# Attention with the next block's k (and first q) products in the tail of the current block, and a second layer whose run 1 multiplies the skip input before its norm

## The chip, the core and the metric

The kernel runs on one core of one Trainium2 chip. The metric is the device time of one execution in microseconds (us). TensorE is PE here (its weight loads are PEld), VectorE is DVE, ScalarE is ACT, GpSimd is POOL, and SyncE (SP) issues the DMAs.

## What is computed

Four conditioned layers follow each other on x of 32 sequences x 64 tokens x 256 channels, all in f32. Layers 0 and 2 are attention and MLP, layers 1 and 3 are selective state-space layers (32 and 64 states) run forward and backward. Of layer 0:

```python
normed = _adaln(x, cond, w_adaln1, b_adaln1)
q = (normed @ wq.T + bq).reshape(B, L, NH, HD)      # 16 heads of 16
k = (normed @ wk.T + bk).reshape(B, L, NH, HD)
v = (normed @ wv.T + bv).reshape(B, L, NH, HD)
attn = softmax(einsum('blhd,bmhd->bhlm', q, k) / scale)
x = x + einsum('bhlm,bmhd->blhd', attn, v).reshape(B, L, D) @ wo.T + bo
x = x + gelu(_adaln(x, cond, w_adaln2, b_adaln2) @ w1.T + b1) @ w2.T + b2
```

Layer 2 has a causal mask and gates on both additions, and its q, k and v have no bias. In layer 1 the part that matters here is `y = scan(...) + Dp * x`, where x is the convolved input; `Dp * x` is the skip input.

## The kernel before, in words

Channels lie on the partitions (256 channels are two chunks of 128), tokens along the free dimension. The 2048 tokens are four blocks of 512, and a block has four pairs of sequences. `attention(l)` is written once for each engine (PE, ACT, DVE, POOL) as a loop over blocks i. Each iteration interleaves three jobs: the attention of block i (`now`), the MLP of block i-1 (`mlp`), and the norm that makes the attention input H of block i+1 (`nxt`). Each engine executes its list strictly in the order written; `attention_steps` lists the same order, so that a name such as `k0@2` stands for a semaphore count. `made(engine, name)` waits for such a count, and `claim(bank, reader)` makes a product wait until the last reader of its PSUM bank is done.

On PE an iteration i of 1 to 3 is: `k0 k1` (L1250, through L1243), `ln2_mean`, `next_mean`, `q0 q1`, `ln2_var`, `v0` (L1262), `score0` (L1278), `v1`, `next_var`, `score1`, `up0` to `up3`, `score2`, `tr0` (a transpose, L1289), `up4`, `av0` (L1304), `up5` to `up7`, `score3`, `tr1`, first half of `down0` (L1326), `av1`, `tr2`, second half of `down0`, `av2`, `tr3`, first half of `down1`, `av3`, second half of `down1`, and `proj0 proj1` (L1243). I call the part up to `up0` the head of the block and the part from `tr1` on its tail. Block 0 has no MLP beside it, so its tail is `tr1 av1 tr2 av2 tr3 av3 proj0 proj1`.

DVE adds `proj` to the residual (L2345 or L2353), makes `ln2_added`, centres, normalises (`ln2_normed` L2366, `ln2_h` L2443) and works on the scores: `seen{p}` (L2379) adds the mask to `score{p}`, then come row maximum, subtraction, and after ACT's exponential the sum and its reciprocal (L2394). POOL expands the keys with the head mask (`kbd{p}`, four instructions, L2713) and multiplies by the reciprocal (`norm{p}`, L2721), for which `tr{p}` waits. ACT evicts k and q (L1828) and v (L1844), squares (L1833), computes the exponentials (L1863), evicts `tr{p}` as `pt{p}` (L1867) for `av{p}` and `av{p}` as `o{p}` (L1873). H is written by DVE's `next_h` (L2482), which waits for `v1` since v is the last reader of the old H. In block 0 of the first layer ACT also copies modulation sums (`site_copied`, L1857).

`pipeline(l)` is layer 1 or 3: eight runs (four blocks, forward and backward), each of 32 or 64 states in four steps. Each step is one DVE scan (L2255); POOL multiplies each finished state (L2678), and PE adds the products up. Work beside the scans (norm, convolution, next inputs) is placed at step numbers by `Plan`. On POOL, `skip` (L2546) makes the skip input in two halves, and `norm` makes `scaled` (L2563) and `h` (L2571). In the odd runs the convolution (L2059) overwrites its input and waits for `skip1`; DVE's `normed` (L2028) waits for `scaled`.

## Time and profile before

| | us |
|---|---|
| median of 3 runs (lowest, highest) | 4480.66 (4478.26, 4488.74) |
| the profiled execution, its own time | 4482.45 |
| its span in the trace | 4480.6 |
| PE busy | 4244.2 (95%) |
| DVE busy | 4059.0 (91%) |
| ACT busy | 3941.2 (88%) |
| POOL busy | 3821.8 (85%) |

The span is what lies between the first and the last recorded instruction; 1.85 us lie around it. The first layer's attention takes about the first 290 us, the second layer's scans run from 290 to 1629 us, the third layer's attention from about 1640 to 1950 us, and the fourth layer to the end. A timeline row has the start, the time of the group and, in brackets, how long the engine had been idle and what released it. TensorE has two clock levels, 2.4 GHz and 1.2 GHz; the column PEclk gives the granted share (1.00 or 0.50 of full speed).

### The profile page before, as it was taken

Reading aid. Unit: us, or ns where it says so; the run is one execution under the profiler, and the core shown is the slowest. Engines: PE = TensorE matmul, PEld = TensorE weight load, DVE = VectorE, ACT = ScalarE, POOL = GpSimd, SP = SyncE. Lnnn points to the kernel's source line nnn. Section 1 sums busy time; section 2 is a strip of 40 time slices with the busy share of each in tenths; the row PEclk is TensorE's granted clock in tenths of the full one; section 3 lists DMA queues with packets and bytes.
Section 4 is the critical chain, followed back from the end, with each engine's and each line's share of the span. In section 5 each row is a group of like instructions: output and inputs, shape, how many; then the busy total and the mean of one; then the engine's idle time right before and its main releaser. Section 6 shows DMA issues by size and latency. Waiting matters only on the chain.

```text
span 4480.6 us, 80902 instructions
## 1 busy us (share of the span) xinstructions
PE 4244.2 (95%) x31358; PEld 3461.6 (77%) x31358; DVE 4059.0 (91%) x3943; ACT 3941.2 (88%) x6176; POOL 3821.8 (85%) x1533
## 2 busy tenths in 40 slices
PE   9999899899899999999999999999999999999998
PEld 5458788788788864468888888888888888888887
DVE  6669999999999977669999999999999999999996
ACT  4569999999999964479989999999999999999995
POOL 3349999899899973259999999999999999999996
PEclk9999999999999999999999999999999999999999
DMA  4012122121121211032232422422422423323221
GB/s 166 1 30 65 61 66 65 53 64 64 53 64 66 64 65 41 1 60 69 94 69 80 82 67 78 82 70 81 87 70 74 79 78 93 65 75 69 72 82 40
DMA packets 241389, 303.33 MB, mean 68 GB/s; under 512 B 116448, under 2 KB 175712, under 8 KB 241008
## 3 DMA queue, kind: packets, MB, share of 16 engines
q1 hardware_dynamic: 241008, 298.15, 23.9%
q8 instruction: 251, 4.11, 0.4%
q14 instruction: 130, 1.06, 0.1%
HBM read 289.84 MB, written 8.26 MB: 67 GB/s over the span
## 4 chain that ended last, share of the span: by engine, by line
PE 41%; ACT 38%; DVE 13%; issue 5%; POOL 3%; DMA 0%; DVEq 0%; SPq 0%; POOLq 0%; ACTq 0%
PE psum L1137 11%; PE psum L1121 10%; ACT weights_c L1744 10%; PE psum L850 8%; ACT work L1765 7%; ACT work L1744 6%; DVE work L2255 6%; ACT weights_c L1765 6%; PE psum L1243 5%; DVE weights_c L2255 3%; PE psum L1118 2%; ACT L1461 2%; ACT modulation L1744 2%; POOL work L2678 1%; PE psum L1326 1%
## 5 line engine op out<-in xcount | busy, mean ns | idle before, releaser
L2678 POOL TENSOR_TENSOR work<-work,weights_a 128x2048 f32<-128x2048 f32 x512 | 1980.7, 3881 | 36.7 <-DVE work L2255 34.2
L2255 DVE TENSOR_TENSOR_SCAN work<-weights_c,psum 128x512 f32<-128x512 f32 x1316 | 1507.2, 1202 | 55.9 <-PE psum L1121 39.1
L1137 PE MATMUL psum<-ident,work 128*128 128x128 f32 x8192 | 1232.7, 274 | 13.1 <-POOL work L2678 12.6
L2678 POOL TENSOR_TENSOR weights_c<-weights_c,weights_a 128x2048 f32<-128x2048 f32 x256 | 990.7, 3879 | 13.8 <-DVE weights_c L2255 12.4
L1121 PE MATMUL psum<-ident,work 128*128 128x128 f32 x5464 | 952.4, 277 | 44.8 <-DVE weights_c L2255 13.3
L1137 PEld LDWEIGHTS psum<-ident,work 128*128 128x128 f32 x8192 | 963.8, 142 | 19.6 <-POOL work L2678 19.1
L1744 ACT ACTIVATE work<-work,decay 128x504 f32<-128x504 f32 x1172 | 819.0, 709 | 46.8 <-DVE weights_c L2255 25.6
L1121 PEld LDWEIGHTS psum<-ident,work 128*128 128x128 f32 x5464 | 659.6, 142 | 237.2 <-issue 130.6
L1121 PE MATMUL psum<-ident,weights_c 128*128 128x128 f32 x4432 | 782.6, 278 | 47.8 <-DVE work L2255 28.0
L2255 DVE TENSOR_TENSOR_SCAN weights_c<-work,psum 128x512 f32<-128x512 f32 x586 | 677.5, 1202 | 23.5 <-PE psum L1121 21.4
L2255 DVE TENSOR_TENSOR_SCAN work<-work,psum 128x512 f32<-128x512 f32 x586 | 675.9, 1201 | 25.2 <-PE psum L1121 16.9
L1121 PEld LDWEIGHTS psum<-ident,weights_c 128*128 128x128 f32 x4432 | 535.5, 142 | 173.0 <-issue 81.1
L1137 PE MATMUL psum<-ident,weights_c 128*128 128x128 f32 x4096 | 619.3, 274 | 9.4 <-POOL weights_c L2678 9.2
L1765 ACT ACTIVATE work<-work 128x512 f32<-128x512 f32 x683 | 486.0, 712 | 13.5 <-PE psum L1326 13.5
L1137 PEld LDWEIGHTS psum<-ident,weights_c 128*128 128x128 f32 x4096 | 483.5, 142 | 13.3 <-POOL weights_c L2678 13.1
L1765 ACT ACTIVATE work<-weights_a,work 128x512 f32<-128x512 f32 x683 | 486.1, 712 | 0.0
L1744 ACT ACTIVATE weights_c<-work,decay 128x504 f32<-128x504 f32 x584 | 409.2, 708 | 21.1 <-DVE work L2255 11.3
L1744 ACT ACTIVATE weights_c<-weights_a,weights_c 128x504 f32<-128x504 f32 x512 | 354.3, 707 | 35.4 <-DVE work L2255 34.3
L1744 ACT ACTIVATE weights_c<-work,weights_c 128x504 f32<-128x504 f32 x512 | 355.3, 708 | 23.9 <-DVE work L2255 23.4
L2255 DVE TENSOR_TENSOR_SCAN weights_c<-weights_c,psum 128x512 f32<-128x512 f32 x292 | 342.1, 1202 | 7.4 <-PE psum L1121 6.0
L1765 ACT ACTIVATE weights_c<-work,weights_c 128x512 f32<-128x512 f32 x384 | 273.1, 712 | 2.4 <-PE psum L1209 2.4
L1765 ACT ACTIVATE weights_c<-weights_a,weights_c 128x512 f32<-128x512 f32 x384 | 272.8, 710 | 0.0
(230 smaller groups left out, 6198.3 us busy)
## 6 DMA issues: line engine op xcount, KB each, us to landing
weights_a<-c_rows SPq DMA_DIRECT2D x384, 512.0 KB, 3.7
work<-b_diagonals SPq DMA_DIRECT2D x240, 128.0 KB, 2.4
weights_c<-b_diagonals SPq DMA_DIRECT2D x112, 128.0 KB, 2.5
b_diagonals<-weights_c SPq DMA_DIRECT2D x1, 4096.0 KB, 18.2
weights_c<-in_L_cond_fwd_in_w SPq DMA_DIRECT2D x8, 512.0 KB, 5.4
weights_c<-in_L_cond_fwd_xproj_w SPq DMA_DIRECT2D x4, 1024.0 KB, 7.0
weights_c<-in_L_cond_bwd_in_w SPq DMA_DIRECT2D x8, 512.0 KB, 5.3
weights_c<-in_L_cond_bwd_xproj_w SPq DMA_DIRECT2D x4, 1024.0 KB, 7.1
```

The lines of the kernel that those rows point to most:

```text
L850: last = nc.tensor.matmul(PS[0:rows, bank, :], weights[k], moving[k], start=(k == 0), stop=(k == len(moving) - 1))
L1118: nc.tensor.matmul(PS[:, bank, SCALED * P:T], buf["dtx"][r % 2][:, SCALED, j * P:(j + 1) * P], buf["diagonal"][:, s // 2 % 2, s % 2, :], s ...
L1121: last = nc.tensor.transpose(PS[:, bank, t * P:(t + 1) * P], buf["scaled"][s % INPUTS][t][:, j * P:(j + 1) * P], IDENT[:, :])
L1137: last = nc.tensor.matmul(PS[:, i, k * P:(k + 1) * P], flat[:, at:at + P], IDENT[:, :], start=begins and k == 0, stop=ends and k == DC - 1 ...
L1243: last = nc.tensor.matmul(PS[:, bank, :], weights[k], moving[k], start=(k == 0), stop=(k == len(moving) - 1))
L1326: last = nc.tensor.matmul(PS[:, 5 + c, :], W2A[:, k, c * P:(c + 1) * P], G[l][:, k, :], start=(k == 0), stop=(k == MLP // P - 1))
L1461: act.add_instruction(mybir.InstLoadActFuncSet(name=nc.get_next_instruction_name(), engine=act.engine, act_func_set_id=which, ins=[], outs ...
L1744: f(seqs[:, :, lo:lo + SEQ - 1], dts[:, :, lo:lo + SEQ - 1], ACT.Exp, scale=rate).then_inc(ss["decay_ready"], 1)
L1765: last = f(buf["scaled"][s % INPUTS][t], buf["dtx"][r % 2][:, t, :], ACT.Copy, scale=weight)
L2255: v.tensor_tensor_scan(buf["ring"][s % RING][:, along, j], buf["decay"][q % DECAYS[l]][:, along], PS[:, 4 + q % LOOKAHEAD, along], 0.0, AL ...
L2678: g.tensor_tensor(state, state, row.unsqueeze(2).broadcast_to([P, T, DC]), ALU.mult).then_inc(ss["prod_ready"], 1)
```

## The change

In both attention layers, for i of 0 to 2, the next block's k products are moved from the head of iteration i+1 into the tail of iteration i: for i of 1 and 2, `k0@i+1` stands between `av1` and `tr2` and `k1@i+1` between `av2` and `tr3`; for i = 0 both stand between `av2` and `tr3`, followed by `q0@1` after `tr3` and `q1@1` after `av3`. These products use PSUM banks 0 and 1. ACT's evictions move with them. The heads are reordered: block 1 has `v0` (bank 6), the two means, `v1` (bank 2), `score0`, `ln2_var`; blocks 2 and 3 have `q0 q1`, the two means, `v0` (bank 6), `score0`, `ln2_var`, `v1`. ACT's square of the next input no longer stands behind the evictions of q. `site_copied(4)` moves on ACT from before `pt2` to behind `o2`. In the second layer's run 1, POOL makes `skip0` and `skip1` after its first and second state, ahead of `scaled`, instead of between `scaled`, `h` and the convolution. No product is added or removed. The lists in `attention_steps` change in the same way and are left out below.

```diff
--- before.py
+++ after.py
@@ -229,7 +229,7 @@
         if norms:
             a += ["square"] if not (first and gated) else []
             v += ["mean", "normed"]
-            g += ["scaled", "skip0", "h", "skip1"] if r % 2 else ["scaled", "h"]
+            g += ["skip0", "skip1", "scaled", "h"] if r == 1 else ["scaled", "skip0", "h", "skip1"] if r % 2 else ["scaled", "h"]
         if head and r % 2 == 0:
             a += ["bc"]
         if r == RUNS:
...
@@ -1247,10 +1283,20 @@
                     def average(name, bank, reads, added):
                         product(name, bank, reads, [MEAN[:, :]], [added[:, 0, :]])
 
-                    def project(name, c, at, bank):
+                    opens, second, more = now and i == 0, i == 1, now and i + 1 < NBLK
+
+                    def project(name, c, at, bank, block=i):
                         o = at * D + c * P
-                        product(f"{name}{c}", bank, by("act", f"{name}{c}"),
-                                [WQKVO[:, k, o:o + P] for k in range(KC)], [H[:, k, :] for k in range(KC)])
+                        claim(bank, (st["act"].semaphore, st["act"].lead(f"{name}{c}@{block}")))
+                        for k in range(KC):
+                            last = nc.tensor.matmul(PS[:, bank, :], WQKVO[:, k, o:o + P], H[:, k, :],
+                                                    start=(k == 0), stop=(k == KC - 1))
+                        last.then_inc(mine.sem(f"{name}{c}@{block}"), 1)
+
+                    def upcoming(name, c, at):
+                        if more:
+                            made("dve", f"next_h@{i}")
+                            project(name, c, at, c, i + 1)
 
                     def values(half, bank):
                         wv = WQKVO[:, :, 2 * D:3 * D].rearrange("p k (h r d) -> p k h r d", r=2, d=HD)
@@ -1332,21 +1378,23 @@
                         if l == 0 and i == 0:
                             site_sums(s, (7, 6, 5)[s % 3])
 
-                    if now:
+                    if opens:
                         behind("out1")
-                        if l == 2 and i == 0:
+                        if l == 2:
                             pe.wait_ge(pipe[1]["pool"].semaphore, pipe[1]["pool"].lead(f"h@{RUNS - 1}"))
+                            pe.wait_ge(dma_w[2], 16 * NW[2])
                         else:
                             made("dve", f"next_h@{i - 1}")
-                        if i == 0:
-                            if l == 0:
-                                pe.wait_ge(dma_qkv, 16 * 4)
-                                pe.wait_ge(dma_small, 16 * 2)
-                            else:
-                                pe.wait_ge(dma_w[2], 16 * NW[2])
+                            pe.wait_ge(dma_qkv, 16 * 4)
+                            pe.wait_ge(dma_small, 16 * 2)
                         for c in range(KC):
                             project("k", c, 1, c)
                         behind("mean")
+                    if now and i > 1:
+                        for c in range(KC):
+                            project("q", c, 0, 2 + c)
+                    if second:
+                        values(0, 6)
                     ahead("in1", "in1")
                     if mlp:
                         if l == 0 and i == 1:
@@ -1358,9 +1406,16 @@
                     if nxt:
                         made("dve", f"next_added@{i}")
                         average("next_mean", 4, by("dve", "next_centred"), NEXT_A[1])
-                    if now:
+                    if opens:
                         for c in range(KC):
                             project("q", c, 0, 2 + c)
+                    if now and i > 1:
+                        values(0, 6)
+                    if second:
+                        values(1, 2)
+                    if now and i > 0:
+                        made("act", f"q1@{i}")
+                        score(0)
                     if l == 0 and i < 0:
                         pe.wait_ge(dma_cond, 16 * 2)
                         site_sums(0, 0)
@@ -1372,10 +1427,11 @@
                     if l == 0 and i == NBLK:
                         site_sums(6, 4)
                     behind("var")
-                    if now:
+                    if opens:
                         values(0, 4)
                         made("act", f"q1@{i}")
                         score(0)
+                    if now and not second:
                         values(1, 2)
                     behind("gate2")
                     if nxt:
@@ -1423,16 +1479,25 @@
                         down(0, 0)
                     if now:
                         attend(1)
+                        if i > 0:
+                            upcoming("k", 0, 1)
                         turn(2)
                     if mlp:
                         down(0, 1)
                     if now:
                         attend(2)
+                        if i == 0:
+                            upcoming("k", 0, 1)
+                        upcoming("k", 1, 1)
                         turn(3)
+                        if i == 0:
+                            upcoming("q", 0, 0)
                     if mlp:
                         down(1, 0)
                     if now:
                         attend(3)
+                        if i == 0:
+                            upcoming("q", 1, 0)
                     if mlp:
                         down(1, 1)
                     if now:
@@ -1822,11 +1887,17 @@
 
                     second_lead = l == 0 and i == NBLK
 
-                    def project(name, dst, bank):
-                        for c in range(KC):
-                            made("pe", f"{name}{c}")
+                    opens, second, more = now and i == 0, i == 1, now and i + 1 < NBLK
+
+                    def project(name, dst, bank, chunks=range(KC), block=i):
+                        for c in chunks:
+                            act.wait_ge(st["pe"].semaphore, st["pe"].lead(f"{name}{c}@{block}"))
                             f(dst[:, c, :], PS[:, bank + c, :], ACT.Identity,
-                              bias=vec(cfg["b" + name], c)).then_inc(done(f"{name}{c}"), 1)
+                              bias=vec(cfg["b" + name], c)).then_inc(mine.sem(f"{name}{c}@{block}"), 1)
+
+                    def upcoming(name, dst, *chunks):
+                        if more:
+                            project(name, dst, 0, chunks, i + 1)
 
                     def square(name, centred, to):
                         made("dve", f"{name}_centred")
@@ -1885,24 +1956,32 @@
                             tables(EXP_LN)
 
                     behind("yt")
-                    if now:
+                    if opens:
                         project("k", KF, 0)
+                    if now and i > 1:
+                        project("q", Q, 2)
+                    if second:
+                        values(0, 6)
                     behind("square")
                     ahead("mirror1", None)
                     if mlp:
                         square("ln2", LN_A[0], LN_A[1])
                     ahead("mirror3", "silu_x")
-                    if now:
+                    if opens:
                         project("q", Q, 2)
+                    if second:
+                        values(1, 2)
                     if nxt:
                         square("next", NEXT_A[0], NEXT_A[1])
+                    if now and i > 1:
+                        values(0, 6)
                     behind("rstd")
                     if mlp:
                         rsqrt("ln2", 7, LN_A[2])
-                    if now:
-                        if i == 0:
-                            act.wait_ge(vbd_zeroed, 1 + l // 2)
+                    if opens:
+                        act.wait_ge(vbd_zeroed, 1 + l // 2)
                         values(0, 4)
+                    if now and not second:
                         values(1, 2)
                     if nxt:
                         rsqrt("next", 4, NEXT_A[2])
@@ -1930,12 +2009,21 @@
                         turned(1)
                         exps(3)
                         outputs(1)
-                        site_copied(4, 6)
+                        if i > 0:
+                            upcoming("k", KF, 0)
                         turned(2)
                         outputs(2)
+                        site_copied(4, 6)
+                        if i == 0:
+                            upcoming("k", KF, 0)
+                        upcoming("k", KF, 1)
+                        turned(3)
+                        if i == 0:
+                            upcoming("q", Q, 0)
+                        outputs(3)
+                        if i == 0:
+                            upcoming("q", Q, 1)
                         site_copied(5, 5)
-                        turned(3)
-                        outputs(3)
                     if i == 1:
                         rates = A1 if l == 0 else A3
                         act.wait_ge(dma_rates, 16 if l == 0 else 16 * 3)
@@ -2588,9 +2676,12 @@
                     if 0 <= r < RUNS and r % 2 == 0:
                         yield from skip(r, done)
                     if norm1:
+                        if r == 1:
+                            yield from skip(r, done)
                         yield from norm(r, plan, done, 2 if head else 4, H, nb, f"z3@{r - 1}" if r > 0 else None,
-                                        between=skip(r, done, (0,), 13))
-                        yield from skip(r, done, (1,), 17)
+                                        between=skip(r, done, (0,), 13) if r > 1 else ())
+                        if r > 1:
+                            yield from skip(r, done, (1,), 17)
                     if ends:
                         yield from norm(r, plan, done, 3, H1B, nb, f"up2@{r - 1}" if r >= 4 else None)
                     if r % 2 and head and r >= 0:
```

## Rows read from the trace of the kernel before

**Rows 1.** The page, section 4: shares of the chain that ended last, by engine.
```profile
PE 41%; ACT 38%; DVE 13%; issue 5%; POOL 3%; DMA 0%; DVEq 0%; SPq 0%; POOLq 0%; ACTq 0%
```
**Rows 2.** Waits of PE, 122 to 181 us: who was waited for, total us, times, longest.
```profile
PE psum L1289 <- POOL work L2721: 1.8, 2, 1.1
PE psum L1304 <- ACT work L1867: 0.4, 1, 0.4
```
**Rows 3.** Timeline of PE, block 2: start us, us, what, count, [idle before, releaser].
```profile
121.90 3.60 PE L1243 MATMUL psum<-work,weights_a 128*128 128x512 f32 x8
125.33 3.60 PE L1243 MATMUL psum<-normed,weights_a 128*128 128x512 f32 x8
...
134.87 2.02 PE L1262 MATMUL psum<-weights_a,normed 128*64 128x128 f32 x32
136.81 1.09 PE L1278 MATMUL psum<-work 64*64 64x256 f32 x16
137.84 2.02 PE L1262 MATMUL psum<-weights_a,normed 128*64 128x128 f32 x32
...
165.95 1.07 PE L1289 MATMUL psum<-ident,work 128*128 128x128 f32 x8 [0.66 <-POOL work L2721]
...
172.17 1.06 PE L1289 MATMUL psum<-ident,work 128*128 128x128 f32 x8 [1.10 <-POOL work L2721]
```
**Rows 4.** Timeline of ACT, block 2: the square of the next block's centred input.
```profile
134.70 1.05 ACT L1833 ACTIVATE work<-work 128x1024 f32<-128x1024 f32 x1
```
**Rows 5.** Timeline of DVE, block 2: `ln2_normed`, `ln2_h`, `next_normed`.
```profile
137.02 1.23 DVE L2366 TENSOR_TENSOR work<-work 128x1024 f32<-128x1024 f32 x1 [0.55 <-ACT work L1839]
...
139.42 1.52 DVE L2443 TENSOR_TENSOR work<-work,modulation 128x1024 f32<-128x1024 f32 x1
...
149.52 1.63 DVE L2366 TENSOR_TENSOR work<-work 128x1024 f32<-128x1024 f32 x1
```
**Rows 6.** Timeline of PE, first layer, tail of block 0, `proj`, `k` of block 1.
```profile
54.52 1.11 PE L1304 MATMUL psum<-work 128*32 128x64 f32 x32 [2.87 <-ACT work L1867]
...
61.57 5.07 PE L1243 MATMUL psum<-work,weights_a 128*128 128x512 f32 x8 [0.84 <-ACT work L1873]
66.47 3.60 PE L1243 MATMUL psum<-normed,weights_a 128*128 128x512 f32 x8
```
**Rows 7.** Timeline of ACT, the same stretch: the six evictions of `site_copied(4)`.
```profile
52.29 1.17 ACT L1857 ACTIVATE modulation<-psum,vectors 128x32 f32<-128x32 f32 x6
```
**Rows 8.** Timeline of DVE, the same stretch: `next_h` of block 0.
```profile
53.41 1.16 DVE L2482 TENSOR_TENSOR normed<-work,modulation 128x1024 f32<-128x1024 f32 x1
```
**Rows 9.** Two windows: busy time (instructions) of each engine, PEclk, DMA share, GB/s.
```profile
54.20:64.30 10.10, 6.89 (x76) 4.57 (x77) 0.37 (x1) 3.52 (x12) 2.58 (x2) 0.50 0.67 206
1696.00:1709.60 13.60, 7.67 (x76) 4.87 (x77) 5.94 (x5) 2.81 (x6) 2.75 (x1) 0.50 0.89 304
```
**Rows 10.** Timeline of PE, third layer, tail of block 0, and `k` of block 1.
```profile
1696.69 1.10 PE L1304 MATMUL psum<-work 128*32 128x64 f32 x32 [2.53 <-ACT work L1867]
1701.08 1.94 PE L1289 MATMUL psum<-ident,work 128*128 128x128 f32 x8 [3.29 <-POOL work L2721]
...
1711.36 3.60 PE L1243 MATMUL psum<-normed,weights_a 128*128 128x512 f32 x8
```
**Rows 11.** Timeline of DVE, the same stretch: `next_h` of block 0.
```profile
1699.21 2.80 DVE L2482 TENSOR_TENSOR normed<-work,modulation 128x1024 f32<-128x1024 f32 x1
```
**Rows 12.** Timeline of POOL, second layer, run 1: `scaled`, then `skip1`.
```profile
468.66 1.91 POOL L2563 TENSOR_TENSOR scratch<-scratch,modulation 128x1024 f32<-128x1024 f32 x1
...
486.87 2.11 POOL L2546 TENSOR_TENSOR work<-work,vectors 128x1024 f32<-128x1024 f32 x1
```
**Rows 13.** Timeline of DVE, the same run: `normed`, then the first convolution instruction.
```profile
471.63 1.22 DVE L2028 TENSOR_TENSOR scratch<-scratch,psum 128x1024 f32<-128x1024 f32 x1 [0.27 <-ACT psum L1500]
...
489.09 0.81 DVE L2059 TENSOR_SCALAR work<-psum,vectors 128x512 f32<-128x512 f32 x1 [2.88 <-POOL work L2546]
```
**Rows 14.** Timeline of POOL, block 2: the four instructions of `kbd2`.
```profile
138.02 3.39 POOL L2713 TENSOR_TENSOR work<-work,head_mask 128x256 f32<-128x256 f32 x4 [4.37 <-PE psum L1278]
```

More of the change, by code:

```diff
@@ L397, in attention_steps @@
         add(act, mlp, *(f"gelu{j}" for j in range(4, 8)))
-        add(act, now, "exp2", "o0", "pt1", "exp3", "o1", "pt2", "o2", "pt3", "o3")
+        add(act, now, "exp2", "o0", "pt1", "exp3", "o1")
+        if i > 0:
+            upcoming(act, "k0")
+        add(act, now, "pt2", "o2")
+        upcoming(act, *(("k0", "k1") if i == 0 else ("k1",)))
+        add(act, now, "pt3")
+        if i == 0:
+            upcoming(act, "q0")
+        add(act, now, "o3")
+        if i == 0:
+            upcoming(act, "q1")
         add(dve, mlp, *sums("x"), "ln2_added")
```

43 lines of the change are left out of this document (35 added, 8 removed).

## The prediction

> **What bounds the kernel now.** I read the chain of work that ended last first: PE and ACT share it, DVE has a third of either [rows 1]. So no engine is the bound alone, and each stage needs its own reading. The change touches two stages (attention in layers 0 and 2) and one run of layer 1's scans; the scan stages otherwise keep every instruction.
>
> In attention, blocks 1 to 3 repeat one pattern. The waits of PE over block 2 show it almost full: 2.2 us in 59, two in the tail before `tr2` (0.66) and `tr3` (1.10), where PE waits for POOL's `norm`, and 0.4 before `av0` [rows 2, 3]. The reader is to see that the tail, which is to take 3.43 us more of PE work per block, has 1.76 us of room. The head has none: `proj` starts at 121.90 and nothing idles up to `up0`. The tail of block 0, without MLP, has more room (a gap of 2.87 us in layer 0, of 3.29 in layer 2), but there PE runs at the lower of its two clocks [rows 6, 9, 10].
>
> **The ledger.** The change removes and adds no product, so PE's work is the same in sum. What it moves, it takes from one place of PE's queue and puts into another. The end of a layer's attention moves by the change of PE's idle time, plus what the clock costs. k is four 512-column products in two chunks, 125.33 - 121.90 = 3.43 us for a set of this size, 1.71 a chunk [rows 3]; q is the same.
>
> **Head of blocks 2 and 3.** From the start of `proj`: `proj` to 3.43, `q` to 6.86, the two means to 8.58 (each half of a chunk, 0.86), `v0` 1.94 (134.87 to 136.81 [rows 3]), `score0` 1.03 (136.81 to 137.84), so `ln2_var` ends at 12.4 instead of at 134.87 - 121.90 = 12.97. It is hardly earlier, because q only takes k's place as cover for DVE's residual. After it come Ln and Exp on ACT. Before, they also stood 0.75 us behind the square (134.70 to 135.75, the variance ready at 134.87 plus a hand-over of 0.2 [rows 4]), and `ln2_normed` began at 137.02, 2.15 after the variance; now about 1.5 after it, at 13.96. From `ln2_normed` to the end of `ln2_h` DVE takes 139.42 + 1.45 - 137.02 = 3.85 us, `seen0` between them [rows 5], so `ln2_h` is made at 17.8 and `up0` can start at 17.9. PE on its side is through `v1`, `next_var` and `score1` at 12.4 + 1.94 + 0.86 + 1.1 = 16.4. So a new wait of 1.5 us stands ahead of `score1` and `up0`: DVE's chain is late next. Behind it 0.2 more goes at `up3` (behind the first gelu) and 0.4 at `tr1`, since `norm1` follows DVE, which gained less than PE. With the 0.4 at `av0`, which stays, that is 2.5 us.
>
> Block 2 fills both tail gaps (1.76): 2.5 against 2.14 (0.38 + 0.66 + 1.10), so it is **0.4 us longer**. Block 3 gives k away and takes none, so it keeps the 1.10 gap and, as `tr1` is late, 0.24 of the 0.66: -3.43 + (2.5 + 1.34 - 2.14) = **-1.7 us**.
>
> **Head of block 1.** k and q are both gone, and DVE's residual is covered by `v0` only: `ln2_mean` at 5.4, `ln2_var` from 10.07 to 10.97. ACT's queue is now `v0`, square, `v1`, square: Ln waits for the second square until 11.35 and `ln2_normed` begins at 12.7, `ln2_h` ends at 16.5. PE is ready at 12.95: a wait of 3.7 us, plus 0.2 and 0.4 as above. The block is -6.86 + 3.43 + (3.67 + 0.2 + 0.38 + 0.39 - 2.14) = **-0.9 us**. Layer 2 does each residual in two DVE instructions, one more of 0.7 us per chunk: 0.4 us of further wait in block 1 and 0.1 in 2 and 3. Sum of the three blocks: **-2.2 us in layer 0, -1.6 in layer 2**.
>
> **Tail of block 0, layer 0.** `site_copied(4)` no longer stands ahead of `pt2`: 1.0 us [rows 7], so `av2` starts at 53.5. But `k0@1` reads H, and `next_h` ends at 53.41 + 1.16 = 54.57 [rows 8]: PE waits until 54.7, and `tr3` is queued behind k. PE's clock is low from 54.2 to 64.3 [rows 9]; it came back 2.8 us after dense products had begun at 61.57 [rows 6]. With the dense k starting at 54.7 I let it come back 2.9 us later, at 57.6: 1.43 us of work are done by then, the other 2.0 end at 59.57. Then `tr3` 0.9 (the work at full clock behind the rows of 172.17), `q0` 1.71, which hides `pt3` on ACT (an instruction of the 1.05 us class [rows 4]), `av3` 0.6 (1.11 at the low clock [rows 6]), `q1` 1.71, which hides `o3`: `proj` starts at 64.55 and ends at 67.98, against 66.47 [rows 6]: **+1.5 us**.
>
> **Tail of block 0, layer 2.** `next_h` runs from 1699.21 to 1702.01 [rows 11], while `tr3` started at 1701.08 [rows 10]. Put ahead of it, k waits for `next_h` until 1702.15 and delays `tr3`, `av3` and `proj` behind it. PE idles 4.4 us instead of 3.29 there. The clock is low from 1696 to 1709.6 [rows 9]; after dense work from 1702.15 I let it return at 1706.2, 4.05 us later (between the 2.8 us of layer 0 and the bound below). k ends at 1707.6, `tr3` 1708.5, `q0` 1710.2, `av3` 1710.9, `q1` and then `proj` from 1712.6 to 1716.0, against 1711.36 [rows 10]: **+4.65 us**.
>
> The two ends of the clock: if it stays low through all of k in both tails, k and q cost up to 1.7 us more in each layer (+3.4); if it does not fall at all, 1.4 less in layer 0 and 2.0 less in layer 2. The rows have it fall while PE idles ahead of `av2`, in work that the change leaves as it is, so I take the middle. The Trainium skill (TensorE: Matmul & The Clock Gate, "What's actually happening") says that the throttled state is the default and activity releases it; by that rule, too, only the idle stretch ahead of k decides, and this case's rows show the fall there. A denser tail would by the rule be the better end, 3.4 us less.
>
> **Run 1 of layer 1.** DVE's first convolution instruction waited 2.88 us for `skip1` [rows 13]; POOL had it behind `scaled` and `h`. With both skips of 2.0 us each ahead of `scaled`, that wait goes. But POOL was full there but for two gaps of 0.64 us ahead of its second and third state, so `scaled` ends 4.1 - 1.3 = 2.8 us later: 468.66 + 1.87 + 2.8 = 473.4 [rows 12]. DVE's `normed`, at 471.63 before, needs it and now starts at 473.45: a new wait of 1.8 us, with two scans that PE and ACT have ready queued behind it. Net 1.8 - 2.88 = **-1.1 us**. The ends: -2.9 if `scaled` is in time, +1.8 if the wait that is removed was only hiding another.
>
> No DMA is moved; SP's queue waits only for scan counts and is not passed.
>
> **Sum.** Layer 0: 1.5 - 2.2 = -0.7. Layer 2: 4.65 - 1.6 = +3.0. Run 1: -1.1. Together +1.2 us on a span of 4480.6, so 4481.8 in the trace and 4483.7 for an execution like the profiled one; that one was 1.8 above the median, so a median of **4481.9 us**. Everything else costs nothing: kbd0 and kbd1 of the next block move under `down1` and `proj`, where POOL was idle.
>
> **A rule against it.** DVE's next `normed` takes 1.63 us beside POOL's `kbd3`, and 1.23 where POOL is idle [rows 5]. `kbd2`, four instructions in 3.39 us [rows 14], started 1.0 us after `ln2_normed`; now `score0` comes earlier and `kbd2` covers `ln2_normed` (+0.4) while `ln2_h`, 1.45 beside POOL, gets free (-0.3). I take 0. The Trainium skill (SBUF — State Buffer, "SBUF: two separate sides") has these two engines share one port pair as an exclusive lock: a VectorE instruction with two SBUF inputs waits for the whole GpSimd instruction in flight. The 0.4 us agree with it; what it would cost at its worst is rival B.
>
> **Rivals.** (A) *The gain is real*: the new head waits do not come, because DVE gets through from `ln2_mean` to `ln2_h` as PE does. For it speaks that DVE idles several times in the head (0.55 before `ln2_normed` [rows 5]); against it, that this chain is of dependent steps, not of busy time. It takes away 6.7 us in layer 0 and 7.3 in layer 2 (3.7 and twice 1.5 each, plus the 0.6 of layer 2), and with `scaled` in time 1.8 more: 4481.9 - 15.8 = 4466.
>
> (B) *Slower by the lock of DVE and POOL*: in each of six heads `ln2_normed` comes while one of `kbd2`'s instructions is in flight and waits for its whole 3.39 / 4 = 0.85 us, on the path to `up0`: 5.1 us, and 4487. It decides if `score0` starts less than 3.4 us ahead of `ln2_normed`; I have them 3.4 apart in block 2 (10.5 and 13.96) and 3.6 in block 1, on the edge. If in run 1 the removed wait also hid another (+2.9), 4490.
>
> (C) *The change does less than it says*: k in the tail is held by its bank (`seen3` must have read banks 0 and 1) or by `next_h`, and PE just idles at another place. In blocks 1 and 2 `seen3` ends within 0.3 us of `av1`, so at most 0.3 a block: 4482.5, not to be told from the forecast.
>
> **Chances.** Forecast with C 0.70, its own range 4477 to 4486; A or most of it 0.17; B or another loss of that size 0.13. The range of 4466 to 4490 reaches to both. A measurement of this kernel can tell about 0.3% (13.4 us) from no change: below 4467.2 is A at its full size, 0.10; above 4494.1 needs more than B, 0.05; within 0.85.
>
> **What would show it.** In PE's timeline: k between `av1` and `tr2` with no gap ahead of `tr2` and `tr3`; new waits of PE for DVE ahead of `score1` (L1278) and `up0`, 1.5 us in blocks 2 and 3 and 3.7 in block 1; `proj` of block 1's head ending 1.5 and 4.65 us later; blocks of 58.0, 59.3 and 57.2 us (58.9 before, at the full clock). In run 1, `skip1` ahead of `scaled`, DVE waiting some 2 us before L2028 and not at L2059. Wrong it would be if PE's head waits are under 0.5 us, if the clock does not fall in the tails, or if the fourth layer, whose instructions are the same, changes its length by more than a few us.

## The result, and the profile after

| | before | after |
|---|---|---|
| median of 8 runs each, in turn on one chip (us) | 4485.01 (4478.26 to 4489.28) | 4492.51 (4485.54 to 4499.36) |
| the profiled execution, its own time | 4482.45 | 4492.14 |
| its span in the trace | 4480.6 | 4490.3 |

The ratio is 1.0019, with an interval of 1.0011 to 1.0028: the change costs 7.5 us, where 1.2 were forecast. The kernel before also came out 4.3 us above the median of its first three runs, so part of the distance to the predicted 4481.9 is the start from which it was counted; 6.3 us are the step's own. The range ended at 4490.0. Counted by the ratio from the first median, the time would be 4489.2; as measured it lies 2.5 us above the range.

The page of the kernel after: its span, the busy times, and section 4, which answers [rows 1].

```profile
span 4490.3 us, 80913 instructions
PE 4250.9 (95%) x31358; PEld 3463.1 (77%) x31358; DVE 4058.2 (90%) x3943; ACT 3942.1 (88%) x6176; POOL 3815.2 (85%) x1533
PE 41%; ACT 38%; DVE 12%; issue 5%; POOL 3%; DMA 0%; DVEq 0%; SPq 0%; POOLq 0%; ACTq 0%
```

The page hardly changes. PE's busy time grows by 6.7 us with the same number of instructions, and no other engine's grows by more than 1 us. That is the first hint: the products did not become more, some of them became slower.

I cut both traces at the starts of DVE's scans, which no step of the change moves. The stages of the two spans, in us:

| stage | before | after | difference |
|---|---|---|---|
| start to the first scan of layer 1 | 289.8 | 291.2 | +1.4 |
| layer 1, run 1 | 170.9 | 174.0 | +3.1 |
| layer 1, the other runs | 1168.8 | 1170.6 | +1.8 |
| last scan of layer 1 to first scan of layer 3 (layer 2) | 320.7 | 327.5 | +6.8 |
| layer 3's scans | 2479.2 | 2475.8 | -3.4 |

The last row needs care. Layer 3 has the same instructions in all kernels here, and their traces show lengths from 2474.6 to 2479.3, six of the thirteen near 2475.8 and four near 2479.2. Both of these occur with the old and with the new order in layer 2, so I don't take the row for an effect of the change. Of the +9.7 us in the spans, the reader should keep the +6.8 of layer 2 and the +3.1 of run 1.

Timeline of PE, after, third layer, from the tail of block 0 (answers [rows 10]) to the lead of layer 3:

```profile
1703.05 1.10 PE L1350 MATMUL psum<-work 128*32 128x64 f32 x32 [2.53 <-ACT work L1938]
1708.43 5.72 PE L1292 MATMUL psum<-normed,weights_a 128*128 128x512 f32 x8 [4.28 <-DVE normed L2570]
...
1719.11 3.60 PE L1279 MATMUL psum<-work,weights_a 128*128 128x512 f32 x8
...
1732.10 1.12 PE L1279 MATMUL psum<-work,mean_weights 128*128 128x512 f32 x2 [1.01 <-DVE work L2449]
1735.53 1.17 PE L1324 MATMUL psum<-work 64*64 64x256 f32 x16 [2.30 <-DVE work L2467]
1736.62 8.71 PE L1279 MATMUL psum<-work,weights_a 128*128 128x512 f32 x16
...
1908.65 1.12 PE L1279 MATMUL psum<-work,mean_weights 128*128 128x512 f32 x2 [1.39 <-DVE work L2449]
1910.09 19.10 PE L886 MATMUL psum<-work,weights_c 128*128 128x512 f32 x40 [0.31 <-ACT work L1742]
```

The same instructions of `up0` to `up3` and of layer 3's lead, before:

```profile
1727.89 7.13 PE L1243 MATMUL psum<-work,weights_a 128*128 128x512 f32 x16
1898.66 17.40 PE L850 MATMUL psum<-work,weights_c 128*128 128x512 f32 x40 [0.31 <-ACT work L1677]
```

Windows of after over three of these places (columns as in [rows 9]):

```profile
1704.00:1716.00 12.00, 7.72 (x26) 3.80 (x20) 4.31 (x4) 2.94 (x5) 4.98 (x5) 0.64 1.01 343
1735.00:1742.00 7.00, 6.47 (x25) 3.06 (x26) 6.93 (x8) 2.99 (x4) 0.35 (x1) 0.76 0.00 0
1908.00:1916.00 8.00, 7.04 (x12) 2.90 (x13) 4.69 (x5) 4.51 (x4) 0.00 (x0) 0.79 0.01 2
```

The first place is the forecast one: k waits 4.28 us for `next_h`. The second and third are not. Behind the new waits of block 1's head the granted clock is 0.76 in the mean of its window (a stretch at 1.2 GHz inside one at 2.4), and `up0` to `up3`, sixteen instructions in the trace, take 8.71 us. At 1910 the first products of layer 3, its lead (forty instructions), meet another low stretch (0.79) and take 19.10.

In the second layer's run 1, DVE's waits in the stretch 452 to 626 us (engine line waited for: us in total, times, longest):

```profile
DVE work L2343 <- PE psum L1157: 5.3, 8, 1.5
DVE scratch L2116 <- POOL scratch L2651: 2.0, 1, 2.0
```

The timeline of DVE there, `normed` and the first convolution instruction, which answer [rows 13]:

```profile
475.50 1.22 DVE L2116 TENSOR_TENSOR scratch<-scratch,psum 128x1024 f32<-128x1024 f32 x1 [1.96 <-POOL scratch L2651]
489.99 0.78 DVE L2147 TENSOR_SCALAR work<-psum,vectors 128x512 f32<-128x512 f32 x1
```

And that of POOL, `scaled`, which answers [rows 12]:

```profile
473.47 1.93 POOL L2651 TENSOR_TENSOR scratch<-scratch,modulation 128x1024 f32<-128x1024 f32 x1
```

`normed` waits 1.96 us for `scaled`, and the convolution no longer waits, both as forecast. But DVE's scans wait 5.3 us for PE in eight places; before it was 2.0 in three. The timeline of PE shows how: the same products at 512 and at 519 us.

```profile
512.40 0.85 PE L1157 MATMUL psum<-ident,weights_c 128*128 128x128 f32 x3
513.04 1.06 PE L1173 MATMUL psum<-ident,work 128*128 128x128 f32 x4
...
519.32 0.49 PE L1157 MATMUL psum<-ident,weights_c 128*128 128x128 f32 x3
519.65 0.60 PE L1173 MATMUL psum<-ident,work 128*128 128x128 f32 x4
```

PE's clock is low in three stretches of run 1 (497.4 to 500.8, 511.0 to 517.9, 528.1 to 531.5); before it was low in one, 491.1 to 497.9.

### The profile page after: what moved, and what is told of

It is laid out like the page before. It is cut to its first block, busy times and chain, and to the rows that moved or that the text cites. A ratio compares the mean times of both kernels' runs of the same rounds, so it can differ in the third digit from the quotient of the medians.

```text
span 4490.3 us, 80913 instructions
## 1 busy us (share of the span) xinstructions
PE 4250.9 (95%) x31358; PEld 3463.1 (77%) x31358; DVE 4058.2 (90%) x3943; ACT 3942.1 (88%) x6176; POOL 3815.2 (85%) x1533
## 4 chain that ended last, share of the span: by engine, by line
PE 41%; ACT 38%; DVE 12%; issue 5%; POOL 3%; DMA 0%; DVEq 0%; SPq 0%; POOLq 0%; ACTq 0%
PE psum L1173 11%; ACT weights_c L1809 10%; PE psum L1157 10%; PE psum L886 9%; ACT work L1830 7%; ACT work L1809 6%; ACT weights_c L1830 6%; DVE work L2343 5%; DVE weights_c L2343 3%; PE psum L1279 3%; PE psum L1154 3%; ACT L1526 2%; POOL work L2769 2%; PE psum L1372 2%; ACT modulation L1809 2%
## 5 line engine op out<-in xcount | busy, mean ns | idle before, releaser
L1173 PE MATMUL psum<-ident,weights_c 128*128 128x128 f32 x4096 | 618.6, 274 | 10.6 <-POOL weights_c L2769 10.3
```

What stands on the lines that cost most here:

```text
L1173: last = nc.tensor.matmul(PS[:, i, k * P:(k + 1) * P], flat[:, at:at + P], IDENT[:, :], start=begins and k == 0, stop=ends and k == DC - 1 ...
```

## The experiments

My theory after the result: *the waits are as forecast, and what they bring along is priced wrongly, namely TensorE's clock in the stretches behind them.* Rivals: the waits themselves add up to more than forecast; or the parts of the change disturb each other. All kernels but e7, e10 and e11 hold the same work as the two given ones; these three add products of no use, called fillers. The experiments share a table that chooses the order by layer, `MODE`, where "new" is the changed kernel's order and "old" the one before. A diff below shows only the line that tells a kernel from its neighbour; lists that change with it, such as POOL's, are left out. Each kernel's median is of 11 runs, and its ratio is taken against the kernel before, run beside it.

### One part at a time

e1 keeps the change of run 1 alone, both attentions have the old order:

```diff
-MODE = {0: 'new', 2: 'new'}
+MODE = {0: 'old', 2: 'old'}
```

e2 keeps both attentions and has the old order in run 1:

```diff
-g += ["skip0", "skip1", "scaled", "h"] if r == 1 else ["scaled", "skip0", "h", "skip1"] if r % 2 else ["scaled", "h"]
+g += ["scaled", "skip0", "h", "skip1"] if r % 2 else ["scaled", "h"]
```

e3 keeps layer 0's attention alone and e4 layer 2's alone, both with the old run 1:

```diff
-MODE = {0: 'new', 2: 'new'}
+MODE = {0: 'new', 2: 'old'}
```
```diff
-MODE = {0: 'new', 2: 'new'}
+MODE = {0: 'old', 2: 'new'}
```

> Only the order of the skip products in run 1 of layer 1 is changed; attention is that of the kernel before. Theory (the skip change is worth about 1 us, and what run 1 lost in the changed kernel's profile is TensorE at 1.2 GHz in that execution): DVE waits about 2 us for POOL's scaled at its normed and not at its first convolution, that convolution starts 0.5 to 1.5 us earlier after the start of run 1 than before (39.0 us), run 1 lasts 169 to 171 us unless the clock falls more often in it, and the whole is within 0.05% of the kernel before (-1 us). Rival (the skip order itself makes run 1 longer): run 1 lasts 174 us again as in the changed kernel, and the whole is 3 us slower.

> Both attention layers as in the changed kernel, run 1 of layer 1 in the old order. Theory (the loss is attention's): the whole is 6 to 9 us slower than before, run 1 lasts 171 us, layer 0 to its last proj is 0.4 us longer, layer 2 from the last scan of layer 1 to the first of layer 3 is 5 to 7 us longer (327 against 320.7). Rival (the skip change carries 3 us of the loss): 3 to 5 us slower than before.

> Only layer 0's attention is changed. Theory (layer 2 has the loss, since there next_h is late; layer 0 is even): within 0.05% of the kernel before, first scan at 290 to 291.5 us against 289.8. Rival (the head waits of blocks 1 to 3 make both layers alike slower): half the loss, 3 to 4 us slower, and the first scan at 293 us.

> Only layer 2's attention is changed. Theory: 5 to 7 us slower than before, all of it between the last scan of layer 1 and the first of layer 3, 4.9 us of it before the end of the first proj (k waits for next_h). Rival (both layers alike): 3 to 4 us slower.

| kernel | median us | ratio (interval) | run 1 | layer 2's stage |
|---|---|---|---|---|
| e1, run 1 alone | 4484.24 | 0.9997 (0.9989 to 1.0006) | 174.1 | 320.7 |
| e2, both attentions | 4491.02 | 1.0017 (1.0008 to 1.0025) | 170.9 | 327.5 |
| e3, layer 0's attention | 4483.79 | 0.9999 (0.9990 to 1.0007) | 170.9 | 320.8 |
| e4, layer 2's attention | 4491.15 | 1.0014 (1.0005 to 1.0023) | 171.2 | 327.5 |

The stages follow their part exactly: 327.5 wherever layer 2's attention is changed and 320.7 where it is not; 174.0 or 174.1 only where run 1 is. The parts don't disturb each other, and the loss that can be measured sits in layer 2. Layer 0's part changes nothing that can be measured, though in the traces of e2 and e3 layer 1 starts at 294.9 and 292.8 us and not by 291.5, as I had expected of e3; the section on layer 0 comes back to this. For run 1, e1's rival came true in the stage: it is 3.2 us longer there too, where I had expected 169 to 171 us. The whole of e1 is not slower all the same; a loss of 3 us is at the edge of what the ratio tells.

### Layer 2: who gets k early

In e5 block 0 keeps its own tail, and only from block 1 on does k move into the tail; block 1 then has the old head.

```diff
-MODE = {0: 'new', 2: 'new'}
+MODE = {0: 'old', 2: 'from1'}
```

> Only layer 2 is changed, and its block 0 takes nothing into its tail: block 1 has k and q in its head as before, blocks 1 and 2 give k away. Stage read: last scan of layer 1 to first scan of layer 3 (320.7 us before, 327.5 with all of layer 2 changed). Theory (block 0's tail, where k waits for next_h and runs at the low clock, and block 1's starved head are the loss): 321 to 323 us, and the whole 0 to 3 us slower than before. Rival (the reordered heads of blocks 2 and 3 lose it): 325 us or more.

The stage took 321.7 us, as expected, and the kernel 4486.19, a ratio of 1.0007 (0.9998 to 1.0016). So 5.7 of the 6.8 us go away when block 0 keeps its tail and block 1 its head; 1.7 of them are the low stretch in the lead of layer 3, which e5 does not have either. From one last `proj` of a block to the next, block 1 was 1.7 us longer than before (3.43 us of k into 1.76 us of room), block 2 was 0.7 longer and block 3 was 1.25 shorter: the steady part of the move brings 1.1 us of loss, not a gain.

e6 is e4 with k of block 1 behind `tr3` and q behind `av3`, so that `tr3` isn't queued behind the wait for `next_h`. The names stand for what follows `av2`, `tr3` and `av3`.

```diff
-FIRST = {2: (('k0', 'k1'), ('q0',), ('q1',))}
+FIRST = {2: ((), ('k0', 'k1'), ('q0', 'q1'))}
```

> Only layer 2 is changed; in block 0's tail k stands behind tr3 instead of ahead of it, and q behind av3. Theory (the moved products themselves fill PE at the low clock, whatever their order; the wait for next_h is only a little longer than the one for tr3 was): stage 326 to 327 us, 0.7 to 1 us less than 327.5. Rival (k, queued ahead of tr3 behind a late next_h, is the whole of the loss): 323 us.

PE, e6, the tail of block 0 and `score1` of block 1:

```profile
1703.61 1.94 PE L1354 MATMUL psum<-ident,work 128*128 128x128 f32 x8 [3.29 <-POOL work L2831]
1705.34 5.13 PE L1306 MATMUL psum<-normed,weights_a 128*128 128x512 f32 x8
...
1714.56 3.60 PE L1293 MATMUL psum<-work,weights_a 128*128 128x512 f32 x8
...
1730.97 1.09 PE L1343 MATMUL psum<-work 64*64 64x256 f32 x16 [2.30 <-DVE work L2489]
1732.06 8.83 PE L1293 MATMUL psum<-work,weights_a 128*128 128x512 f32 x16
```

The wait of k is gone and `tr3` waits its old 3.29 us, but `proj` starts only 0.7 us earlier than in the changed kernel (82.7 us behind the last scan, against 83.3). The 4.28 us wait was thus not the price of the tail: what k and q put ahead of `proj` is 6.9 us of work, and only the gaps of the old tail take some of it back. The stage took 325.2 us, 2.3 less than after (expected: 0.7 to 1 less); 1.7 of that is the low stretch in the lead of layer 3, which e6 doesn't have. The ratio is 1.0016 (1.0007 to 1.0025), not told apart from the changed kernel's.

### Layer 2: does the wait of the head cost the clock?

e7 is e4 with eight 128-column products ahead of `score1` in block 1, into a PSUM tile that nobody reads. They add 1.95 us of work of no use (sixteen instructions in the trace) into a wait of 2.30.

```diff
+                    if second or late:
+                        made("dve", f"ln2_squares@{i}")
+                        for _ in range(8 if second else 0):
+                            nc.tensor.matmul(PS[:, 5, 0:P], MEAN[:, :], MEAN[:, :], start=True, stop=True)
                     if now:
                         score(1)
```

> Only layer 2 is changed, and PE gets eight small products without a use (128 columns, MEAN by MEAN) ahead of score1 of block 1, where it waited 2.3 us for DVE. Theory (the starved head also lets the clock fall, and the four up products that follow pay 1.6 us for it): the clock stays at its upper level there, up0 to up3 take 7.1 instead of 8.7 us, and the stage is 1 to 1.8 us shorter than 327.5. Rival (the wait costs only itself): up0 to up3 as before, stage 327.5.

Timeline of PE, e7, the same place and the lead of layer 3:

```profile
1730.69 1.95 PE L1468 MATMUL psum<-mean_weights 128*128 128x128 f32 x16
1733.16 1.09 PE L1343 MATMUL psum<-work 64*64 64x256 f32 x16 [0.52 <-DVE work L2493]
1734.25 7.46 PE L1293 MATMUL psum<-work,weights_a 128*128 128x512 f32 x16
...
1906.75 17.41 PE L900 MATMUL psum<-work,weights_c 128*128 128x512 f32 x40 [0.31 <-ACT work L1764]
```

Windows of e7 over the two places (columns as in [rows 9]):

```profile
1732.00:1739.00 7.00, 6.48 (x33) 3.25 (x33) 6.93 (x7) 2.60 (x4) 0.00 (x0) 1.00 0.00 0
1905.00:1913.00 8.00, 7.38 (x17) 3.23 (x18) 4.51 (x5) 4.21 (x4) 0.00 (x0) 1.00 0.01 2
```

`score1` starts as late as ever, the clock stays at 1.00, and the ups take 7.46 us instead of 8.71 (I had expected 7.1). All four traces with this wait and no filler in layer 2 (after, e2, e4, e6) have the low stretch, and it starts 100.4 to 100.7 us behind the last scan of layer 1 in each. Up to the wait e7's clock ran as e6's did: in both the low stretch of the tail ended 76.5 us behind that scan. So the filler is what differs. Work without use made the stage shorter: 324.7 us against 327.5. Of the 2.8 us, 1.0 is block 1 (the ups gain 1.25, and 0.25 of it goes back into waits further on); 1.7 are the lead of layer 3, whose low stretch is absent as well. That second one is not a wait's doing: the 1.39 us wait in front of it stands in every kernel (1.38 in e7's). The low stretch is there in the traces of after, e2 and e4, which reach the lead 274.3 us behind the last scan of layer 1, and not in those of e5, e6 and e7, which reach it at 270.3, 273.8 and 273.2. I can say that it goes with where the stage's work falls in time, and not why. The ratio of e7 is 1.0004 (0.9995 to 1.0013), which overlaps that of e4, 1.0014 (1.0005 to 1.0023): the gain is seen in the stage, and the whole time doesn't settle it.

### Layer 0 with the same products

e10 is e3 with such products in all three heads; the diff is against e7's line.

```diff
-for _ in range(8 if second else 0):
+for _ in range(8 if second else 5):
```

> Layer 0's attention as in the changed kernel, with products without use (they write a PSUM tile that nobody reads) ahead of score1: 8 of them in block 1, 5 each in blocks 2 and 3; layer 2's attention and run 1 as in the kernel before. Theory (the wait of score1 lets TensorE's clock fall, and the ups pay): with TensorE at work during the 2.30 us wait the first ups of block 1 take about 7.1 us in place of the 8.9 of the changed kernel, and the last projection of layer 0 ends near 237.5 us (before 239.8, changed kernel 240.2). Rival (the low clock in block 1 has another cause): ups stay near 8.9 us and the last projection ends at 240 or later. The whole: between 0 and 3 us less than before.

Timeline of PE, e10, block 1, and below it the window of e10 over the tail and middle of block 0 (columns as in [rows 9]):

```profile
87.87 1.09 PE L1343 MATMUL psum<-work 64*64 64x256 f32 x16 [0.52 <-DVE work L2493]
88.95 7.46 PE L1293 MATMUL psum<-work,weights_a 128*128 128x512 f32 x16
```
```profile
37.50:61.40 23.90, 22.70 (x174) 19.27 (x173) 16.41 (x16) 8.48 (x21) 8.49 (x8) 0.50 0.37 141
```

The first half of the expectation held: the ups took 7.46 us instead of 8.93, and block 1 was 58.18 us long (71.94 to 130.12, from `proj` to `proj`), where the changed kernel had 60.2 and the forecast was 58.0. That the filler did it isn't shown here, since e2, with the same wait and no filler, has 7.46 and 58.18 as well. The second half failed: the last `proj` of layer 0 started at 247.0 us, not 237.5. The window says where it went: in block 0, whose instructions are those of e3 and of the changed kernel, the clock was low from 37.5 to 61.4 without a break. Traces taken apart in this way, in us:

| kernel | block 0: first `k` to end of `proj` | blocks 1 to 3: to last `proj` |
|---|---|---|
| layer 0 old: before | 49.72 | 173.15 |
| layer 0 old: e1 | 50.21 | 173.17 |
| layer 0 old: e4 | 50.08 | 173.15 |
| layer 0 old: e8 | 49.71 | 173.17 |
| layer 0 old: e9 | 50.43 | 173.15 |
| layer 0 old: e5, e6 and e7 | 54.97 | 173.17 |
| layer 0 new: after | 50.02 | 173.61 |
| layer 0 new: e3 | 51.34 | 172.57 |
| layer 0 new: e2 | 56.43 | 171.58 |
| layer 0 new, filler: e10 | 57.75 | 171.55 |
| layer 0 new, filler: e11 | 57.79 | 171.57 |

Block 0 has a short and a long form under either order. Blocks 1 to 3 are 1.6 us shorter than before with the clock up (e2, e10, e11), 0.6 shorter in e3 and 0.5 longer in after, where the clock fell behind `score1`. e2 also shows that the wait alone doesn't decide: it has no filler, and no low stretch there. What else decides is open.

### Run 1: how many skips ahead of `scaled`

e8 has both skips behind `scaled` and ahead of `h`; e9 has one ahead of `scaled` and one behind it. Attention is as before in both.

```diff
-["skip0", "skip1", "scaled", "h"]
+["scaled", "skip0", "skip1", "h"]
```
```diff
-["skip0", "skip1", "scaled", "h"]
+["skip0", "scaled", "skip1", "h"]
```

> Attention as in the kernel before; in run 1 of layer 1 POOL makes both skips right behind scaled and ahead of h. DVE's normed then has no wait for POOL, and the first convolution waits for h and its product, 0.8 us less than the 2.88 of before. Theory by waits alone: run 1 lasts 170.1 us (170.9 before, 174.0 in the changed order). Rival (the clock sets run 1's length: where the stall lies against the clock's falls decides): run 1 lasts 168 or 172 us or more, with one clock fall or three in it, whatever the waits say.

> The attention is that of the kernel before; in run 1 of the second layer one skip product stands ahead of scaled and one behind it (before: both behind it, after: both ahead of it). Theory (waits set run 1): scaled's product ends half as far back as in the changed kernel, so that normed on VectorE waits some 1 us less than the 1.96 us of the changed kernel, and the first convolution product on TensorE, which waited 2.88 us in the kernel before, waits some 0.9 us; run 1 takes 168.9 us, 2.0 less than the 170.9 before. Rival (the granted clock sets run 1): any product moved ahead shifts the stretches at low clock, as in the changed kernel with three falls, and run 1 takes 172 us or more although the wait is shorter. The whole: 2 us less than before, 0.04%, within what can be told, so the stage and its clock decide and not the ratio.

DVE's waits in run 1, for e8 and then for e9:

```profile
DVE work L2365 <- PE psum L1171: 3.7, 4, 1.7
DVE scratch L2138 <- ACT psum L1583: 0.3, 1, 0.3
```
```profile
DVE work L2365 <- PE psum L1171: 2.3, 4, 1.4
```

Timeline of DVE, e9, `normed`:

```profile
472.04 1.22 DVE L2138 TENSOR_TENSOR scratch<-scratch,psum 128x1024 f32<-128x1024 f32 x1 [0.25 <-ACT psum L1583]
```

The window from 484 to 530 us, for before, after and e9 in this order (columns as in [rows 9]):

```profile
484.00:530.00 46.00, 37.40 (x261) 31.74 (x260) 42.86 (x47) 37.74 (x61) 41.27 (x19) 0.93 0.17 58
```
```profile
484.00:530.00 46.00, 37.82 (x246) 32.68 (x244) 42.75 (x47) 36.00 (x58) 37.69 (x18) 0.87 0.17 55
```
```profile
484.00:530.00 46.00, 37.56 (x274) 31.09 (x275) 45.31 (x50) 39.98 (x65) 42.07 (x20) 1.00 0.18 58
```

Run 1 took 170.0 us in e8 (expected 170.1) and 168.5 in e9 (expected 168.9): neither `normed` nor the convolution waits for POOL in e9, and DVE is busy 45.31 of 46 us. The whole runs gave ratios of 1.0006 (0.9997 to 1.0014) and 1.0000 (0.9991 to 1.0009), so the 2.3 us are seen in the stage and not in the time. By its waits alone the changed order was worth 1.1 us, and its run 1 took 4.2 more than that, in the trace after and in e1's alike. The granted clock differs as well: 0.93 before, 0.87 in after and 1.00 in e9. That the clock is the whole cause is not shown: in e8 DVE's scans waited 3.7 us for PE in a run 1 without any low stretch. Why the clock fell three times in the changed order is open too. PE's idle spans in that stretch are much the same in after (the longest 1.51, 1.41, 1.32, 1.29 us) and in e9 (1.51, 1.44, 1.40, 1.32), and only the first has the falls. I tried no filler there, since a useless product would have needed a free PSUM bank between the scans.

### The gaining parts together

e11 is layer 0 of e10, layer 2 as before, and run 1 of e9.

> The parts that gained by the waits, put together: layer 0's attention as changed with the products without use ahead of score1, layer 2's attention as before, run 1 with one skip product ahead of scaled. Theory (parts add up): 2.3 us from layer 0 and 2.0 us from run 1, so 4 us below the kernel before, a ratio of 0.9991, and the last layer as before. Rival (an earlier start of layer 1 only shifts where the clock falls in the scans, which gives the gain back): ratio 1.0000 or above, with the first scan of layer 1 earlier but the stages behind it longer by as much.

DVE, e11, run 1:

```profile
532.63 2.33 DVE L2369 TENSOR_TENSOR_SCAN work<-weights_c,psum 128x512 f32<-128x512 f32 x2 [0.15 <-PE psum L1171]
535.47 1.22 DVE L2369 TENSOR_TENSOR_SCAN work<-weights_c,psum 128x512 f32<-128x512 f32 x1 [0.50 <-PE psum L1171]
```

4482.79 us, a ratio of 0.9999 (0.9990 to 1.0007), where 0.9991 was expected: no faster than before by any measurement made here. Its trace had the long block 0 and, in run 1, one low stretch (528.6 to 532.0) that e9's did not have, with DVE's waits above and 169.6 us instead of 168.5. So the gains of single stages are real in the traces and as large as the differences that the clock makes between traces. Nothing tried here beats the kernel before by an amount that can be measured.

## Why the prediction was wrong

The step that failed is the term for blocks 1 to 3 of layer 2: -1.6 us in the prediction, +1.9 measured. Of the 3.5 us between them, 2.7 are TensorE's clock, which fell in two places that the sum had at full clock. The other terms follow in the order of the sum.

**The ledger and the head.** Right in the main. The "new wait of 1.5 us" ahead of `score1` in blocks 2 and 3 was 1.40, released by DVE's `seen0`; in block 1, the wait of 3.7 was 1.01 ahead of `next_var` and 2.30 ahead of `score1`. Timeline of PE, after, block 2 (beside [rows 3]):

```profile
131.78 2.02 PE L1308 MATMUL psum<-weights_a,normed 128*64 128x128 f32 x32
133.73 1.09 PE L1324 MATMUL psum<-work 64*64 64x256 f32 x16
...
140.28 1.09 PE L1324 MATMUL psum<-work 64*64 64x256 f32 x16 [1.40 <-DVE work L2467]
```

Timeline of DVE, `ln2_normed` and `ln2_h` (beside [rows 5]):

```profile
137.30 1.62 DVE L2454 TENSOR_TENSOR work<-work 128x1024 f32<-128x1024 f32 x1 [1.07 <-ACT work L1910]
140.10 1.22 DVE L2531 TENSOR_TENSOR work<-work,modulation 128x1024 f32<-128x1024 f32 x1
```

`ln2_normed` starts 14.19 us behind `proj` (forecast 13.96), and from there to the end of `ln2_h` it is 4.02 us (forecast 3.85), so `up0` starts at 18.26 and not at 17.9. Blocks 2 and 3 of layer 0 took 59.4 and 57.5 us (59.3 and 57.2), and with the clock up blocks 1 to 3 were worth 1.6 us, against 2.2 forecast: each block was sized 0.2 us too short.

**Tail of block 0, layer 0.** The waits right, the clock wrong, and to the kernel's benefit. Timeline of PE, after (beside [rows 6]), then the window of the first row of [rows 9]:

```profile
54.22 3.70 PE L1292 MATMUL psum<-normed,weights_a 128*128 128x512 f32 x8 [0.48 <-DVE normed L2570]
...
62.89 3.60 PE L1279 MATMUL psum<-work,weights_a 128*128 128x512 f32 x8
```
```profile
54.20:64.30 10.10, 10.08 (x60) 5.12 (x61) 0.00 (x0) 6.19 (x18) 6.83 (x10) 1.00 0.72 226
```

The clock was 1.00 where it was 0.50 before, and the block was 0.3 us longer, not 1.5. But the other traces with this tail had 1.3, 1.5 and 2.8 us more than the old form of like length (51.34 against 50.08, 56.43 and 57.75 against 54.97), so that the forecast of 1.5 lies inside what they show, if traces of like length are the right pairs.

**Tail of block 0, layer 2.** Right: k waited 4.28 us (4.4), and `proj` ended 4.9 us later against the last scan (4.65). The sentence that k "delays `tr3`, `av3` and `proj` behind it" was right in fact and misleading as a reason: e6 took that delay away and got 0.7 us.

**Blocks 1 to 3 and the lead, layer 2.** This is the step that failed. Forecast -1.6; measured +0.8, +0.7, -1.3 and +1.7 in the lead, +1.9 in all. Of the 3.5 us between them, the low stretch behind `score1` is 1.0 (block 1 took 59.68 us in after and 58.67 in e7) and the one in the lead 1.7; the rest, some 0.8 us, is again 0.2 to 0.3 a block. The sentence that failed is "only the idle stretch ahead of k decides". I priced the clock only in the tails, where it was low before, and treated the new waits of the heads as their own length. A wait of 2.3 us cost 2.3 and then 1.25 in the work behind it, of which 1.0 stayed in the block. For the 1.7 in the lead the sum had no term, and what brings that low stretch stays open.

**Run 1.** The two waits were right (1.8 forecast, 1.96; the 2.88 gone). The net was -1.1 by them and +3.1 in the trace, with a lower clock, though here no run ties the clock to a wait or the 4.2 us to the clock alone. With e1's ratio of 0.9997 this step does not account for the measured slowdown; layer 2's does (e4, 1.0014).

**The rivals.** (A) fell: the head waits came in full. (B) was not it: `ln2_normed` took 1.62 us where it takes 1.23 alone, so the overlap with `kbd` cost 0.39 us and not 0.85, and `ln2_h`, now free of POOL, took 1.22 instead of the 1.52 of [rows 5] (the prediction's 1.45 counts to the start of the next instruction). The net of the two, 0.17 a block, is what the prediction took as 0. The Trainium skill (SBUF — State Buffer, "SBUF: two separate sides") has the two engines share a port pair as an exclusive lock, so that the second waits for the first one's instruction; no run here shows a wait for a whole one, and the 0.39 agree with part of one. (C) was no cause: nothing waits for its bank in the tails. What ended on the slow side was none of the three but a mechanism for which the prediction had a term, in other places. The sum with what is now known: layer 0 -0.7 and +1.1 more, layer 2 +3.0 and +3.8 more, run 1 -1.1 and +4.2 more, together +10.3 for this one trace, less 3.4 by layer 3's other length; and 2.8 more in the lead of layer 1 (1.0) and its other runs (1.8), which no term covered: 9.7, the growth of the span. The prediction's bound for what can be told, 0.3%, was also too coarse: the interval here is 0.09% to either side.

## What to carry to other kernels

Price a new wait on TensorE at two ends: its length alone, and its length with the dense products right behind it at the lower of the two clocks the trace shows (here 1.25 us behind a wait of 2.30 in layer 2; in layer 0 the same wait had a low stretch in the traces of after and e3 and none in e2's, and the waits of 1.40 in after had none). Before moving work out of a full stretch, ask what the stretch does with the hole: block 1 of layer 2 gave away 6.9 us of work and took 3.4, and even with the clock held up (e7) it was only 0.2 us shorter (58.67 against 58.86), since its head waits for DVE's dependent steps. And where the whole is worth some 0.1%, judge each edit by its stage in the trace, and look at a stage in several traces before believing one.

## What the hardware showed unexpectedly

- The same instructions had two lengths from one trace to another. Block 0 of layer 0 in the new order took 50.02 us in one trace and 57.75 in another; the second ran at 0.50 from 37.5 to 61.4 us with PE shown as busy for 22.70 of 23.9 us, the first at 0.93 over 36.5 to 60.5 (busy for 20.51 of 24 us; a product takes longer at 0.50, so the two busy times are not the same work). The Trainium skill (TensorE: Matmul & The Clock Gate, "What's actually happening") has the clock low by default and released by activity. The filler of e7 agrees with that; the window of e10, in which PE hardly stopped and the clock stayed low, does not show such a release.
- Work of no use made a stage 2.8 us shorter (e7, 327.5 to 324.7).
- A low stretch can appear or vanish 175 us behind the edit: in the lead of layer 3 it cost 1.7 us in after, e2 and e4, and was absent in e5, e6 and e7, with the same wait of 1.4 us in front.
